# Attention of a fused audio tower: logits and values in 64x64 quarters, and the softmax maximum taken by bf16 folds

## The reference, cut to what matters

```python
# text: 16 x 746 tokens of 128; video: 64 videos x 12 frames x 128; 2 heads of 64
t  = layer_norm(text_embeds, ln1_g, ln1_b)
vd = layer_norm(video_embeds, ln1_g, ln1_b)
q = (t @ Wq.T + bq).reshape(T, Nw, 2, 64)
k = (vd @ Wk.T + bk).reshape(V, Fr, 2, 64)
v = (vd @ Wv.T + bv).reshape(V, Fr, 2, 64)
logits = einsum("avhd,bthd->abhvt", k, q) / sqrt(64)
weights = softmax(logits, axis=3)          # over the 12 frames of one video
attn = einsum("avhd,abhvt->abhtd", v, weights)...mean(axis=0)   # over the 64 videos
o = attn @ Wo.T + bo
...
```

## Time and profile before

| | us |
|---|---|
| median of 3 runs (lowest, highest) | 2869.18 (2860.5, 2879.31) |
| the profiled execution, its own time | 2875.36 |
| its span, first to last instruction | 2873.7 |
| mean granted TensorE clock | 0.913 of 2.4 GHz |
| attention stage, from the trace | 1334 to 1984: 650 |

### The profile page before, as it was taken

How to read it: one execution, slowest core, us unless ns; L and a number is a source line. 1 busy time by engine, 2 the same in 40 slices (tenths; PEclk the granted TensorE clock), 3 DMA queues, 4 the chain that set the end, 5 groups by cost and what they waited for, 6 DMA issues and landing times. The chain is left out here.

```text
span 2873.7 us, 50470 instructions
## 1 busy us (share of the span) xinstructions
PE 2438.6 (85%) x17384; PEld 2251.1 (78%) x17384; DVE 1647.4 (57%) x3842; ACT 1040.1 (36%) x2242; POOL 783.8 (27%) x761
## 2 busy tenths in 40 slices
PE   7699898999814787886999999997407999999998
PEld 3488888888713677785999999996307999999998
DVE  1655454555582344466888888886995334334343
ACT  2433233333202444442232223223442444444443
POOL 0000000000015444402666666666760000000000
PEclk9899999999755898898999999998855999999999
DMA  7000000000301111100000000000000000000000
GB/s 176 0 1 1 2 1 2 1 1 1 91 12 38 33 31 29 32 4 1 1 1 0 0 0 0 0 1 1 0 0 0 7 11 11 5 11 11 11 11 12
DMA packets 42094, 39.57 MB, mean 14 GB/s; under 512 B 7800, under 2 KB 35944, under 8 KB 41576
## 3 DMA queue, kind: packets, MB, share of 16 engines
q1 hardware_dynamic: 36072, 25.70, 3.6%
q0 software_dynamic: 5888, 12.07, 1.6%
HBM read 25.34 MB, written 12.41 MB: 13 GB/s over the span
## 5 line engine op out<-in xcount | busy, mean ns | idle before, releaser
L1338 DVE SCALAR_TENSOR_TENSOR h<-banks,wt,h 128x128 f32 (+3 forms) x768 | 210.5, 344 | 390.1 <-PE banks L1426 390.1
L1426 PE MATMUL banks<-w,rb 128*128 128x128 f32 (+1 forms) x3072 | 360.9, 274 | 0.0
L1426 PEld LDWEIGHTS banks<-w,rb 128*128 128x128 f32 (+1 forms) x3072 | 355.4, 189 | 0.0
L1404 ACT ACTIVATE rb<-banks,b 128x384 f32<-128x384 f32 (+1 forms) x512 | 258.1, 575 | 197.8 <-PE banks L1452 197.4
L1693 PEld LDWEIGHTS banks<-qT,w 128*128 128x128 f32 x2304 | 273.9, 193 | 15.5 <-DVE qT L1607 1.9
L1670 POOL TENSOR_TENSOR t<-eb 128x768 f32<-128x768 f32 x96 | 220.5, 2297 | 228.5 <-ACT eb L1658 228.5
L1712 PEld LDWEIGHTS banks<-eb,w 128*128 128x128 f32 x2304 | 268.8, 193 | 14.5 <-DVE eb L1627 6.8
L1712 PE MATMUL banks<-eb,w 128*128 128x128 f32 x2304 | 275.3, 276 | 4.9 <-DVE eb L1627 4.6
L1693 PE MATMUL banks<-qT,w 128*128 128x128 f32 x2304 | 274.5, 276 | 0.7 <-DVE qT L1607 0.7
L1069 POOL DMA_INDIRECT xg<-xs,rowu x184 | 182.8, 994 | 191.8 <-PE banks L1183 127.3
L1365 POOL TENSOR_TENSOR e_xlo<-t_xT,e_xh 128x384 fp32r<-128x384 f32 x32 | 32.5, 1017 | 620.3 <-ACT e_xh L1383 620.3
(11 more groups left out here) (302 smaller groups left out, 4919.4 us busy)
## 6 DMA issues: line engine op xcount, KB each, us to landing
out<-h SPq DMA_DIRECT2D x16, 320.0 KB
xs<-r_xl SPq DMA_DIRECT2D x16, 192.0 KB, 2.8
h<-in_xT SPq DMA_DIRECT2D x4, 750.0 KB, 15.4
h<-in_xT SPq DMA_DIRECT2D x4, 749.0 KB, 18.4
xg<-xs,rowu POOLq DMA_INDIRECT x184
xs<-r_xl SPq DMA_DIRECT2D x16, 128.0 KB
w<-in_L_ffn_w1T SPq DMA_DIRECT2D x1, 1024.0 KB
xs<-r_xl SPq DMA_DIRECT2D x16, 53.0 KB
```

The source lines that it names most:

```text
L1338: last = nc.vector.scalar_tensor_tensor(out=k.h[0:n, b, c, :], in0=k.psf[0:n, o:o + P], scalar=gate(i, c, par, e, n), in1=k.h[0:n, b, c, : ...
L1404: nc.scalar.activation(gb[:, (u % 2) * fh + f, s * 384:s * 384 + NFREE[s]], k.ps[:, n % 4, 0:NFREE[s]], func, bias=b1[:, e * fh + f:e * fh ...
L1426: last = nc.tensor.matmul(k.psf[0:n, o:o + P], gb[:, (u % 2) * fh + f, c * P:c * P + n], w2[:, e * fh + f, :], start=(f == 0), stop=(f == ...
```

## The change

Only `video_phase`, `attention_phase` and the norm ahead of them change. The line numbers in this section are those after.

1. **Quarters.** `Kbd` and `Vbd` become `Kt` and `Vd`, without the zeros. Each of the 12 matmuls of a chunk becomes two of 64x64 weights (L1713, L1721), one for each head. In one chunk the logits use the two quarters on the array's diagonal and the values of the chunk four earlier the other two; after every four chunks they change places (`place`). Logits and values alternate frame by frame in one block.
2. **Maximum.** ACT copies the negated logits as bf16 into the chunk's own buffer of exponentials (L1669), and DVE takes the minimum by four folds of 768, 384, 128 and 128 bf16 (L1614 to L1619).
3. **Distances.** The multiply is now for chunk n-2, the values for n-4, the output product for n-5 and its bias for n-6. The shift of chunk n-1 is in PE's step n, behind the block and behind the slot's work. The exponential is three instructions of 512, each with its own signal. `eb` and `den` have four buffers.
4. **ACT for DVE.** The norm and the query bias move from DVE to ACT (L1636, L1642).
5. All steps are written out; before, the steps of six of the eight pairs were a loop.

```diff
             def _(dve):
...
+                for n in range(NCH + 7):
+                    o = n - 6
+                    if 0 <= o < NCH:
+                        dve.wait_ge(o_ps, o + 1)
+                        nc.vector.tensor_tensor(big[:, o, :], k.ps[:, 7, 0:P], k.bo1[:, :], ALU.add).then_inc(o_ready, 1)
...
+                    if n < NCH:
+                        c = coarse(n)
+                        dve.wait_ge(c_ready, n + 1)
+                        for step, w in enumerate((6, 3)):
+                            nc.vector.tensor_tensor(c[:, 0:w, :], c[:, 0:w, :], c[:, w:2 * w, :],
+                                                    ALU.min).then_inc(folded, 1)
+                            dve.wait_ge(folded, 3 * n + step + 1)
+                        nc.vector.tensor_tensor(c[:, 0, :], c[:, 0, :], c[:, 1, :], ALU.min).then_inc(folded, 1)
+                        dve.wait_ge(folded, 3 * n + 3)
+                        nc.vector.tensor_tensor(nm[:, n % 2, :], c[:, 0, :], c[:, 2, :], ALU.min).then_inc(m_ready, 1)
+                    w = n - 2
+                    if 0 <= w < NCH:
...
             def _(act):
...
+                for n in range(NCH + 4):
+                    a = n - 4
+                    if a >= 0:
+                        act.wait_ge(a_ps, a + 1)
+                        nc.scalar.activation(aT[:, a % 2, :], k.ps[:, 6, 0:P], ACT.Copy).then_inc(a_ready, 1)
+                    if slot(n):
+                        nt.move(act, *slot(n), 7, k.g1[:, 0:1], k.b1n[:, 0:1])
+                    if slot(n - 1):
+                        query(*slot(n - 1), 7)
+                    e = n - 1
+                    if 0 <= e < NCH:
+                        for s in range(3):
+                            act.wait_ge(shifted, 3 * e + s + 1)
+                            nc.scalar.activation(eb[:, e % 4, s * FB:(s + 1) * FB], lbanks(e)[:, s * FB:(s + 1) * FB],
+                                                 ACT.Exp).then_inc(e_ready, 1)
+                    if n < NCH:
+                        act.wait_ge(l_ps, n + 1)
+                        nc.scalar.activation(coarse(n), lbanks(n), ACT.Copy, scale=-1.0).then_inc(c_ready, 1)
+                    if slot(n + 1):
+                        norm(*slot(n + 1))
...
             def _(pe):
...
+                    for v in range(FR):
+                        if logits:
+                            if v % FB == 0 and n >= 2:
+                                pe.wait_ge(e_ready, 3 * (n - 2) + v // FB + 1)
+                            for hd in range(2):
+                                last = nc.tensor.matmul(
+                                    lbanks(n)[place(n, hd), v, :], k.Kt[half(hd), v, :],
+                                    qT[half(hd), n // NC % 2, (n % NC) * P:(n % NC + 1) * P],
+                                    start=(v % FB == 0), stop=True, skip_group_check=True)
...
+                        if values:
+                            for hd in range(2):
+                                last = nc.tensor.matmul(
+                                    k.ps[half(hd), 6, 0:P], k.Vd[place(a, hd), v, half(hd)],
+                                    eb[place(a, hd), a % 4, v, :], start=(v == 0), stop=(v == FR - 1))
...
+                    now, before, o = slot(n), slot(n - 1), n - 5
+                    if now or before:
+                        if o >= 1:
+                            pe.wait_ge(o_ready, o)
+                        if before:
+                            query(*before, 7)
+                        if now:
...
+                            nt.turn(pe, *now, 7)
+                    if 1 <= n <= NCH:
+                        pe.wait_ge(m_ready, n)
+                        for s in range(3):
+                            nc.tensor.matmul(lbanks(n - 1)[:, s * FB:(s + 1) * FB, :], k.identb[:, :],
...
```

More of the change, by code:

```diff
@@ L1510, in _ @@
                     ps = k.ps[:, 2 + s, 0:GW].rearrange("p (v a) -> p v a", a=NV)
[L1511 to L1513 removed]
+                    nc.vector.tensor_scalar(k.Kt[:, s * 6:(s + 1) * 6, :], ps, k.bk[:, 0:1], None, ALU.add)
                 for s in range(3):
@@ L1517, in _ @@
                     ps = k.ps[:, 4 + s, :].rearrange("p (v d) -> p v d", d=C)
[L1518 to L1524, removed]
+                    nc.vector.tensor_tensor(k.Vd[:, s * 4:(s + 1) * 4, :], ps,
+                                            k.bv[:, None, :].to_broadcast([P, 4, C]), ALU.add).then_inc(laid, 1)
+                dve.wait_ge(laid, 3)
+                nc.vector.tensor_scalar(k.Vd, k.Vd, 1.0 / NV, None, ALU.mult).then_inc(laid, 1)
+                dve.wait_ge(laid, 4)
             @block.scalar
@@ L1578, in attention_phase, with lbanks @@
         slots = {1: 2, 3: 3, NC + 1: 0, NC + 3: 1}
         big = k.big[:].rearrange("p b c d -> p (b c) d")
-        def lbanks(j):
-            o = 3 * (j % 2) * 512
+        def lbanks(n):
+            o = 3 * (n % 2) * 512
             return k.psf[:, o:o + FR * P].rearrange("p (v t) -> p v t", t=P)
-        def slot(i, j, last_pair):
-            g = slots.get(j)
-            if g is None or (g < 2 and last_pair):
-                return None
-            return (i, g) if g >= 2 else (i + 1, g)
@@ L1592, in over_steps, with coarse, half @@
[L1592 to L1600, removed]
+        def coarse(n):
+            return eb[:, n % 4].rearrange("p v t -> p (v t)").bitcast(BF16)[:, 0:FR * P].rearrange("p (v t) -> p v t", t=P)
+        def half(x):
+            return slice(x * NV, (x + 1) * NV)
@@ L1602, in attention_phase, with place, slot @@
+        def place(n, hd):
+            return half(hd if n // 4 % 2 == 0 else 1 - hd)
+        def slot(n):
+            i, g = n // ST, slots.get(n % ST)
+            if n < 0 or n >= NCH or g is None:
+                return None
+            i += g < 2
+            return (i, g) if i < PAIRS else None
         with nc.Block() as block:
@@ L1604, in _ @@
             def _(dve):
[L1605 to L1627, removed]
@@ L1638, in _ @@
[L1638 to L1644, removed]
                 dve.wait_ge(counted, NCH)
@@ L1648, in _, with norm @@
             def _(act):
[L1649 to L1658, removed]
+                def norm(i, g):
+                    for j in range(GC):
+                        c = (g % 2) * GC + j
+                        at = i * ST + (g // 2) * NC + c
+                        last = nc.scalar.activation(nt.xl[:, g, j, :], k.h[:, i * 2 + g // 2, c, :], ACT.Identity,
+                                                    scale=k.rstd[:, at:at + 1], bias=k.mean[:, at:at + 1])
+                    last.then_inc(nt.normed, 1)
@@ L1660, in _, with query @@
+                def query(i, g, bank):
+                    act.wait_ge(q_ps, i * 4 + g + 1)
+                    nc.scalar.activation(qT[:, g // 2, (g % 2) * GW:(g % 2 + 1) * GW], k.ps[:, bank, 0:GW],
+                                         ACT.Identity, scale=0.125, bias=bq8[:, 0:1]).then_inc(q_ready, 1)
+                for g in range(2):
+                    norm(0, g)
                 for g in range(2):
                     nt.move(act, 0, g, 6 + g, k.g1[:, 0:1], k.b1n[:, 0:1])
-                over_steps(act, step)
+                act.wait_ge(q_bias, 1)
@@ new lines, in _ @@
+                for g in range(2):
+                    query(0, g, 4 + g)
+                for n in range(NCH + 4):
[18 more added lines that the diff above has]
+                        norm(*slot(n + 1))
```

148 lines of the change are left out of this document (62 added, 86 removed).

## The result

| | before | after |
|---|---|---|
| median of 4 runs each (lowest, highest), us | 2868.67 (2860.5, 2879.31) | 3092.48 (3083.19, 3098.14) |
| ratio, 95% interval | | 1.0775 [1.073, 1.0819] |
| span of the profiled execution, us | 2873.7 | 3096.3 |
| mean granted TensorE clock | 0.913 | 0.875 |
| attention stage, us | 648.8 | 872.6 |

A forecast was written before the change was run, and what follows sets the result against it. PE's matmul pairs bound the kernel before; after, a ring of waits would. Stage terms 796 + 44 + 20 - 15 gave 845 us against 650, so +195 on 2875.4, 3070, stated as 3065; range 2840 to 3260.

The forecast's parts named there:

- a group of six steps: Attention steps, four of six with a turn or query: 50.1 us, or 53.1 at 8.85 a step with POOL's interference.
- the port: DVE's folds and POOL's additions, both reading SBUF, take turns: 0.5 us a step, bounds 0 to 1.6.
- PE idle ahead of L323 and L1692, released by L1605: Sign: PE waits before turn and query for DVE's output bias, some 2 us in 60 steps, over 100 in all.
- Slot steps: Attention steps in which PE also does a turn or query: about 9 us from one turn to the next.
- The ring: Closed chain of waits: PE's turn or query, shift, ACT's exponentials and copy, DVE's folds, reciprocal, multiply, bias: 9.1 us.
- PE's block: A step's 96 quarter load-and-matmul pairs for logits and values on PE: 5.33 us, with loads one after the other.
- The serial rival: Quarters run serially on PE: block 10.7 us, step 12.1, PE bound, time 3380 us; chance 0.11.
- The folds: DVE's four bf16 folds for the maximum: 1.35 us a step, priced by bytes; by elements 2.06.
- The rival without a port and with a block of 2.7: Folds slip in beside POOL and PE's block is faster: 7.8 us a step, 2965 us; chance 0.11.
- The clock: Rival: PE's idling lowers its clock for most of the stage: block 9 us, step 10.3, time 3210; chance 0.10.
- The sum: Attention stage: 796 us with slots, 44 for last plain steps, plus 20, less 15: 845, so +195.
- Each engine at its own sum: Rival: attention step set by the fullest resource, 5.6 us if the bias is not late: 2770 us; chance 0.08.

The follow-up runs named there:

- block twice: The changed kernel with PE issuing each step's whole block of logits and values matmuls twice: stage 903.2 us, ratio to before 1.0879.
- the two quarters: The changed kernel with logits and values always on the same two quarters, never the other two: stage 890.3 us, ratio to before 1.085, one run.
- the light POOL: The changed kernel with POOL's four additions for a chunk's softmax sum replaced by a single one: stage 757.6 us, ratio to before 1.0364.
- both edits: The changed kernel with DVE reducing logits from PSUM (no ACT copy, no folds) and output bias ahead of reciprocal and multiply: stage 545.4 us, ratio to before 0.9626.

## Why the prediction was right, and where its terms were off

Predicted was 3065, measured 3092; the mechanism is the one forecast. That the number came so close is in part luck: in a group of six steps the port cost 6.1 us more than I took, and other terms together 4.7 less. Point by point:

- **PE idle ahead of L323 and L1692, released by L1605**: 227 us where over 100 was said, 4 us each where I said 2, since the block is shorter than 5.3. **The stage** of 872.6 is in 800 to 880. **DVE idle** ahead of the first fold: 3.0 a step where over 2 was said. Slot steps are 9.95 and 10.2 where I said about 9.
- **The ring**: shown. Each link taken out gives time back: reciprocal and multiply 147 us, the order of copy and exponential 247, copy and folds 280. Work added outside it (block twice) costs 34. One link was not moved by itself in any run: PE's shift behind the turn or query. That it belongs to the ring is read from the rows of the slot step above.
- **PE's block** failed as a step: I took 5.33, and it is 2.6 at the 2.4 GHz level. The error was the sentence that loads of 64 columns follow one another; the loads of different quarters run together too. The Trainium skill (TensorEngine Tiling (Array Packing), Theoretical Speedup) gives up to 2 for a dimension of 64 or less; the product for both, my estimate from that table, is 4. The trace agrees with it: 8 quarter pairs in 0.22 us, which at one whole pair in 0.11 us would take 0.88. A chunk needs twice as many of them, so the block is halved. The serial rival is excluded by the same rows. Its effect on a group of six steps was mis-sized as well: I had about 3.3 us between the two blocks (50.1 against 6 x 7.8), the two quarters show 0.9.
- **The folds** by themselves: 1.36 for 1.35, by bytes and not by elements. The Trainium skill (VectorE: DVE Perf Modes, the perf-mode tier table) gives a bf16 tensor_tensor in SBUF twice the rate of an f32 one. The trace of the light POOL agrees: 0.56 us for 768 bf16 against 0.54 for 384 f32.
- **The port** (DVE's folds beside POOL's additions): mis-sized. Taken 0.5, bounds 0 to 1.6, measured 2.9 - 1.36 = 1.5. I argued that two short folds fit in gaps; they start when the one before them ends, while POOL is in its tree, so three or four of them meet an addition. The rival without a port and with a block of 2.7 was right on the block and wrong on the port.
- **Exponentials, query bias, copy, reciprocal, multiply**: 1.43 to the copy's start for 1.65, 0.58 for 0.61, 1.47 for 1.45, 0.94 and 1.76 as before. The turn's 0.33 and the query's 0.65 stand in none of the rows that I named for them; from their start to the shift's they took 0.38 and 0.75. A slot step is some 0.5 under its terms: 9.1 + 1.5 = 10.6, and the medians are 9.95 and 10.2. The exponentials are 0.2 of it; the rest lies in signals and overlaps that I did not separate.
- **The clock**: it fell to 0.84 in the stage, as the rival said it could, but what it slows is mostly not on the path: of the 74 stretches of the stage at the lower level 60 begin within 1.5 us behind the end of a stall of PE, when the turn or the query has mostly run, and what they slow is the block. The medians of six steps sum to 54.5 us and their mean to 54.9, so that steps like the one of 10.95 above cost some 0.4 a group, 6 us in the stage.
- **The sum**: a group of six was 53.1 and is 54.5. The port adds 6.1; the block takes off 1, by the two quarters, and the slot terms 2. The other 1.7 lies in plain steps, where waits overlap, and stays unresolved.
- **Each engine at its own sum**, the rival on the other side, had 5.6 us a step and decided at whether the bias comes late. Here it did. With the ring opened by order alone it is what happens, 5.77 us a step. The 5.50 of both edits belongs to other work on DVE, so its being near 5.6 is chance.

## What to carry over

Write the chain of a semaphore wait backward through each engine's program order: one late instruction (a bias behind a multiply) or one early wait (an exponential ahead of a copy) closes a ring which costs more than all the work the change saves. A kernel in which no engine is full, and two wait for each other, wants its instructions in another order before it wants fewer of them. Price every DVE operation that has both inputs in SBUF with POOL's operation beside it.

## What the runs showed of the hardware

- f32 matmuls on all four 64x64 quarters run together, loads included: four pairs start in 0.11 us, on two quarters two.
- A bf16 fold in SBUF takes turns with POOL's f32 additions as an f32 multiply does; the fold of 384 grows most, from 0.36 to 1.03. POOL's 384 addition grows with it, from 1.00 to 1.19, and beside the f32 multiply to 2.39.
- Behind a stall of about 4 us PE's turn or query mostly still ran at the 2.4 GHz level, and the block behind it began at the 1.2 GHz level (two pairs each of logits and values in 0.21) and was back at 2.4 GHz before its end. Doubling PE's work raised the granted clock from 0.84 to 0.94 and left the slot steps as they were.
